# Context and mask rows loaded and masked one round earlier, in four buffers instead of two

## The chip, the core and the metric

The kernel runs on one core of a Trainium2 chip. The core has five engines with instruction streams of their own: TensorE (PE; its weight loads are shown apart as PEld), VectorE (DVE), ScalarE (ACT), GpSimd (POOL) and SyncE (SP). Here SyncE issues all transfers (DMA) between the device's memory and the core's own memory, SBUF. The engines wait for each other by semaphores. The metric is the device time of one execution in microseconds (us).

## What is computed

Sixteen sequences of 128 channels by 256 positions pass four layers, each added to its input:

```python
x = x + _L0_xattn_ref(ctx, ctx, _layernorm(x), ssm_kernel, D, 8)      # long convolution of key-value products
x = x + _L0_ffn_ref(_layernorm(x), gate_w, gate_b, val_w, val_b, out_w, out_b)   # quantised gated FFN
x = x + _L1_xattn_ref(_layernorm(x), ctx, mask, mask, Wq, bq, Wk, bk, Wv, bv)    # masked cross attention, 16 heads
x = x + _L1_ffn_ref(_layernorm(x), Wc, temperature, genes, Wd, Wu, norm_w, scale)  # top 32 of 512, weighted sum
```

The change concerns the third layer. Keys and values are projections of the context `ctx`, and positions are masked:

```python
q = einsum('oc,bct->bot', Wq, target) + bq
k = einsum('oc,bcs->bos', Wk, source) + bk
v = einsum('oc,bcs->bos', Wv, source) + bv
dot = mask * (q . k / sqrt(HEAD_DIM)) - (1 - mask) * NEG
out = (softmax(dot) * mask) @ v
```

The kernel multiplies the context with the mask row once (`ctx_m`), and takes the biases times the mask.

## The kernel before, in words

A first part prepares weights and begins the long convolution. Then every engine runs a loop over `m`. In each pass an engine does one step of many stages, each for another batch: the first stages for batch `m`, the last ones for batch `m - 12`. The order of the calls in each engine's loop is written out by hand, and an engine executes strictly in that order; a step that waits holds all behind it. The outer products of the convolution (`later_products`, L886, with L273 on TensorE) still run in the passes until about 205 us.

The way of batch `b` through the context steps, before the change:

- SyncE, `load_context(m - 6)`: after `write_attention` (L753) and `load_max_rows` (L742) of its pass, it issues the load of the context into `ctx_m[b % 2]` (L694) and of the mask row, spread over 128 partitions, into `mask_b[b % 2]` (L695). SyncE's passes run ahead of the others by about one. At the end of its pass stand `load_stacked_qk` (L726 to L735) and `load_x` (L686).
- GpSimd, `mask_context(m - 5)`: waits for both loads and multiplies them in place (L985). It stands between `chosen_weights` (L1027) and `output_scale`, ahead of `gate_times_value` (L963, two halves).
- TensorE, `project_qk(m - 5)`: keys from `ctx_m` (L432) and queries from the normalised x2 (L433), in the middle of its pass; at the end of the next pass `project_v(m - 6)` (L445, and L446 with the mask row).
- VectorE, `bias_and_mask_qk` (L1489, L1490): adds biases and applies the mask row, right behind `inverse_denominators` (L1510, L1512).
- GpSimd, `split_qk(m - 5)`: splits queries and keys into three bf16 parts (L39 to L45), after which come `add_attention` (L1011, L1013), `normalise_x1` (L910 to L915), `down_times_xr` (L1035) and `normalise_x3` (again L910 to L915).

Others that are named later: TensorE forms the products for the row maxima (L461), whose maxima VectorE takes (L1499), and the scores (L477), whose exponentials ScalarE takes (L1223). The rows of maxima go to the scores by a transfer (L742). TensorE transposes xq (L377, L378) and the normalised x3 (L511), and multiplies values (L490). VectorE opens the gate of the FFN (L1447). L963 needs this result.

Of the kernel before, what the change touches and what calls it, by code (L numbers as in the profile page):

```python
# [25 lines left out]
P = 128  # L26
# [21 lines left out]
def build(nc, a, out):  # L48
    B, C, L = a["x"].shape
# [4 lines left out]
    QB, UNITS = B // 4, 4 * H  # L54
    QK_SCALE = 1.0 / float(HD) ** 0.5
# [19 lines left out]
    with ExitStack() as ctx:  # L75
# [88 lines left out]
        ctx_m = [sb(f"ctx_m{k}", [P, L]) for k in range(2)]  # L164
        mask_b = [sb(f"mask_b{k}", [P, L]) for k in range(2)]
# [78 lines left out]
        def _(pe):  # L244
# [179 lines left out]
            def project_qk(b):  # L424
                if not live(b):
                    return
                if b == 0:
                    pe.wait_ge(s("w_T_taken"), 7)
                pe.wait_ge(s("ctx_m_ready"), b + 1)
                pe.wait_ge(s("xn2_ready"), b + 1)  # L430
                take6("qk", b)
                pe.matmul(X6[:, L:2 * L], wqkvT[:, 1, :], ctx_m[b % 2][:], start=True, stop=True)  # L432
                pe.matmul(X6[:, 0:L], wqkvT[:, 0, :], xn2, start=True, stop=True).then_inc(s("qk_bank_ready"), 1)  # L433

            def project_v(b):
# [7 lines left out]
                for sh in range(KL):  # L443
                    cols = slice(sh * P, (sh + 1) * P)
                    pe.matmul(X7[:, cols], ctx_m[b % 2][:, cols], wqkvT[:, 2, :], start=True, stop=False)  # L445
                    mm = pe.matmul(X7[:, cols], mask_b[b % 2][:, cols], bv0[:], start=False, stop=True)  # L446
# [150 lines left out]
        def _(sp):  # L597
# [90 lines left out]
            def load_context(b):  # L688
                if not live(b):
                    return  # L690
                if b >= 2:
                    sp.wait_ge(s("v_bank_ready"), b - 1)
                    sp.wait_ge(s("x6_free"), turn6["qk", b - 2])
                sp.dma_start(ctx_m[b % 2][:], a["ctx"][b]).then_inc(s(f"ctx{b % 2}_loaded"), 16)  # L694
                sp.dma_start(mask_b[b % 2][:], bass.AP(a["mask"].tensor, b * L, [[0, P], [1, L]])).then_inc(  # L695
                    s(f"ctx{b % 2}_loaded"), 16)
# [93 lines left out]
            for m in range(B + 14):  # L790
# [3 lines left out]
                load_context(m - 6)  # L794
# [6 lines left out]
                load_stacked_qk(m - 7)  # L801
                load_x(m)
# [5 lines left out]
        def _(pool):  # L808
# [171 lines left out]
            def mask_context(b):  # L980
                if not live(b):
                    return
                k = b % 2
                pool.wait_ge(s(f"ctx{k}_loaded"), 32 * (b // 2 + 1))
# [60 lines left out]
            for m in range(B + 12):  # L1045
# [7 lines left out]
                mask_context(m - 5)  # L1053
# [9 lines left out]
                split_qk(m - 5)  # L1063
                add_attention(m - 9)
# [256 lines left out]
        def _(dve):  # L1321
# [160 lines left out]
            def bias_and_mask_qk(b):  # L1482
                if not live(b):
                    return
                k = b % 2
# [159 lines left out]
```

## Time and profile before

| | |
|---|---|
| three runs | 626.14, 622.75, 619.33 us; median 622.75 |
| profiled execution | 624.76 us, span in the trace 622.9 us |
| mean granted TensorE clock | 0.923 of full speed |
| busy: PE | 489.1 us, 79% of the span |
| busy: DVE | 478.0 us, 77% |
| busy: POOL | 401.1 us, 64% |
| busy: ACT | 346.2 us, 56% |

The span is from the first to the last instruction of the trace, and the execution's own time lies 1.9 us above it. Busy shares are means over stages with different limits, so they don't tell by themselves what bounds the kernel. An idle time in brackets behind a row of the timeline is that just before the instruction, with what ended it. A granted clock of 1.00 is 2.4 GHz, 0.50 is 1.2 GHz, and values between are stretches with both.

### The profile page before, as it was taken

The numbers are of one execution on the slowest core, as the hardware profiler recorded it, in microseconds if no ns is written. First come the engines' busy times: TensorE is split into PE (matmuls) and PEld (weight loads), VectorE is DVE, ScalarE is ACT, GpSimd is POOL, SyncE is SP. The second block draws the span as 40 slices with busy tenths as digits, with TensorE's granted clock in tenths as the row PEclk, the third lists the DMA queues.
The fourth block names the chain that finished last, engine by engine and source line by source line (L and its number), as shares of the span: only waits on it lengthen the run. The fifth ranks groups of instructions, "written<-read, shape, count | busy, mean of one in ns | idle before, by whom it ended". The sixth has DMA issues, their size and how long they took to land.

```text
span 622.9 us, 11624 instructions
## 1 busy us (share of the span) xinstructions
PE 489.1 (79%) x3617; PEld 279.7 (45%) x3633; DVE 478.0 (77%) x885; ACT 346.2 (56%) x578; POOL 401.1 (64%) x711
## 2 busy tenths in 40 slices
PE   1676778888788788978989888899987987888463
PEld 1455656666565443444444444444433433333121
DVE  4563658888789876799999999999988868874441
ACT  1246723332221375777877878778865657776321
POOL 6787487798997567577787787785654643432321
PEclk9987979999998897999999999999988879997855
DMA  6940100020624155453563455455565454411100
GB/s 216 373 92 6 29 17 18 10 44 0 117 73 62 30 107 136 88 104 106 89 132 99 89 136 114 78 134 92 103 143 109 86 135 103 87 30 29 46 8 17
DMA packets 92178, 54.31 MB, mean 87 GB/s; under 512 B 14851, under 2 KB 91844, under 8 KB 92118
## 3 DMA queue, kind: packets, MB, share of 16 engines
q1 hardware_dynamic: 92118, 53.58, 38.4%
q8 instruction: 29, 0.48, 0.3%
q14 instruction: 31, 0.25, 0.1%
HBM read 35.64 MB, written 17.42 MB: 85 GB/s over the span
## 4 chain that ended last, share of the span: by engine, by line
POOL 22%; issue 22%; DVE 15%; DVEq 15%; PE 14%; POOLq 9%; ACT 2%; DMA 1%; SPq 0%; ACTq 0%
POOL kv L886 8%; DVE w_int L1499 4%; PE bank L490 3%; DVEq L1540 3%; DVEq L1550 2%; DVEq L1408 2%; POOL yT L843 2%; DVEq L1457 2%; DVE best L1551 2%; DVEq L1533 2%; POOL w_raw L963 2%; POOLq L914 2%; DVE st L1409 2%; DVEq L1436 2%; PE pair L477 1%
## 5 line engine op out<-in xcount | busy, mean ns | idle before, releaser
L1499 DVE TENSOR_REDUCE w_int<-pair 128x4 f32<-128x1024 f32 x128 | 155.6, 1216 | 17.2 <-PE pair L461 16.8
L1223 ACT ACTIVATE cT<-pair 128x1024 f32<-128x1024 f32 x128 | 130.9, 1023 | 57.2 <-PE pair L477 55.4
L273 PE MATMUL pair<-kv,toep 128*128 128x256 f32 x384 | 106.5, 420 | 29.5 <-POOL kv L886 15.3
L273 PEld LDWEIGHTS pair<-kv,toep 128*128 128x128 f32 x384 | 75.9, 209 | 50.3 <-issue 21.5
L886 POOL TENSOR_TENSOR kv<-cT 128x512 f32<-128x512 f32 x64 | 66.1, 1041 | 19.0 <-PE pair L273 12.9
L461 PE MATMUL pair<-KS,w_raw 54*128 54x256 bf16 x512 | 51.8, 282 | 29.6 <-DVE w_int L1499 29.4
L490 PE MATMUL bank<-cT,v_aug 128*32 128x256 f32 x1024 | 72.8, 405 | 0.0
L1361 DVE TENSOR_TENSOR prod<-pair,qT 128x512 f32<-128x512 f32 x64 | 44.3, 691 | 29.8 <-PE pair L273 25.0
L477 PE MATMUL pair<-w_raw,KS 57*128 57x256 bf16 x512 | 52.3, 284 | 13.0 <-ACT cT L1223 5.7
L461 PEld LDWEIGHTS pair<-KS,w_raw 54*128 54x128 bf16 x512 | 16.1, 96 | 73.4 <-DVE w_int L1499 59.8
L1368 DVE TENSOR_REDUCE yT<-prod 128x64 f32<-128x512 f32 x64 | 43.9, 686 | 6.3 <-issue 0.4
L1541 DVE MATCH_REPLACE8 toep<-best,toep 128x512 f32<-128x512 f32 x64 | 43.3, 676 | 0.6 <-issue 0.6
L1172 ACT ACTIVATE w_raw<-bank,st 128x512 f32<-128x512 f32 x32 | 22.0, 687 | 34.2 <-PE bank L383 34.2
L963 POOL TENSOR_TENSOR w_raw<-w_raw 128x512 f32<-128x512 f32 x32 | 40.3, 1275 | 0.0
L382 PE MATMUL bank<-wgvT,ctx_all 128*128 128x512 bf16 x112 | 35.6, 389 | 5.8 <-ACT ctx_all L1196 1.9
L1188 ACT ACTIVATE w_raw<-w_raw,st 128x512 f32<-128x512 f32 x32 | 21.3, 714 | 33.6 <-DVE st L1462 33.6
L477 PEld LDWEIGHTS pair<-w_raw,KS 57*128 57x128 bf16 x512 | 17.2, 96 | 50.5 <-ACT cT L1223 31.8
L490 PEld LDWEIGHTS bank<-cT,v_aug 128*32 128x32 f32 x1024 | 28.0, 113 | 26.1 <-issue 15.5
L1551 DVE MAX8 best<-toep 128x8 f32<-128x512 f32 x48 | 33.4, 695 | 4.2
L39 POOL CAST w_int<-w_int 128x512 bf16<-128x512 f32 (+1 forms) x32 | 13.1, 411 | 34.8 <-DVE w_int L1499 21.5
L519 PE MATMUL bank<-wcT,qT 128*128 128x512 f32 x64 | 34.1, 658 | 0.5 <-ACT qT L1237 0.5
L913 POOL TENSOR_TENSOR st<-st,half_neg 128x1 f32<-128x1 f32 x48 | 26.7, 555 | 7.0
(163 smaller groups left out, 996.1 us busy)
## 6 DMA issues: line engine op xcount, KB each, us to landing
w_raw<-scr_q SPq DMA_DIRECT2D x32, 192.0 KB
KS<-scr_k SPq DMA_DIRECT2D x32, 192.0 KB
scr_q<-w_int SPq DMA_DIRECT2D x16, 192.0 KB, 2.5
scr_k<-w_int SPq DMA_DIRECT2D x16, 192.0 KB, 2.6
scr_o<-qT SPq DMA_DIRECT2D x64, 36.0 KB
yT<-in_x SPq DMA_DIRECT2D x4, 512.0 KB, 7.4
ctx_all<-in_ctx SPq DMA_DIRECT2D x4, 512.0 KB, 7.8
x_b<-in_x SPq DMA_DIRECT2D x16, 128.0 KB, 5.2
```

Source lines behind the costliest of these rows:

```text
L273: mm = pe.matmul(bank[:, lh * n:(lh + 1) * n], toep[:, h, (lh - sh) * P:(lh - sh + 1) * P], rhs[:, sh, :], start=(sh == 0), stop=(sh == lh))
L461: mm = pe.matmul(M[:, at:at + L], QS[b % 3][rows, g, th * P:(th + 1) * P], KS[b % 3][rows, g, :], start=True, stop=True)
L477: mm = pe.matmul(SC[:, at:at + L], KS[b % 3][rows, g, sh * P:(sh + 1) * P], QS[b % 3][rows, g, :], start=True, stop=True)
L490: mm = pe.matmul(O[32 * jj:32 * jj + 32, 0:L], v_aug[b % 2][:, sh, 4 * q + jj, :], probs[(2 * q + jj // 2) % 4][:, jj % 2, sh * L:(sh + 1) ...
L886: pool.tensor_tensor(kv[u % 2][:], ch.unsqueeze(3).broadcast_to(shape), ch.unsqueeze(2).broadcast_to(shape), ALU.mult).then_inc(s("kv_read ...
L963: pool.tensor_tensor(h, h, val[half], ALU.mult).then_inc(s("hid_ready"), 1)
L1223: act.activation(probs[g % 4].rearrange("p j l -> p (j l)"), SC[:], ACT.Exp).then_inc(s("scores_free"), 1)
L1361: dve.tensor_tensor(prod[:], banks[2 + u % 2][:].rearrange("p (r j i) -> p r j i", j=HD, i=HD), qh.unsqueeze(2).broadcast_to([P, KL * QB, ...
L1368: mm = dve.tensor_reduce(yT[:, q].rearrange("p s b c -> p (s b) c")[:, :, heads], prod[:], AX.X, ALU.add)
L1499: dve.tensor_reduce(neg_max[:, :, 2 * g:2 * g + 2].rearrange("p t j -> p j t"), M[:].rearrange("p (j t s) -> p j t s", t=KL, s=L), AX.X, A ...
L1541: mm = dve.match_replace(left, best[:, 8 * r:8 * r + 8], logits[b % 2] if r == 0 else left, GONE)
L1551: dve.max(best[:, 8 * r:8 * r + 8], left)
```

## The change

Context and mask row get four buffers each. The load moves to the end of SyncE's pass, before `load_x`, and is for batch `m - 4` instead of `m - 6`. The mask product moves on GpSimd from ahead of the third outer product to behind `split_qk`, and is for batch `m - 4` instead of `m - 5`. The waits before the load and before the product are adapted to four buffers.

```diff
+    NC = 4
-        ctx_m = [sb(f"ctx_m{k}", [P, L]) for k in range(2)]
-        mask_b = [sb(f"mask_b{k}", [P, L]) for k in range(2)]
+        ctx_m = [sb(f"ctx_m{k}", [P, L]) for k in range(NC)]
+        mask_b = [sb(f"mask_b{k}", [P, L]) for k in range(NC)]
...
             def load_context(b):
                 if not live(b):
                     return
-                if b >= 2:
-                    sp.wait_ge(s("v_bank_ready"), b - 1)
-                    sp.wait_ge(s("x6_free"), turn6["qk", b - 2])
-                sp.dma_start(ctx_m[b % 2][:], a["ctx"][b]).then_inc(s(f"ctx{b % 2}_loaded"), 16)
-                sp.dma_start(mask_b[b % 2][:], bass.AP(a["mask"].tensor, b * L, [[0, P], [1, L]])).then_inc(
-                    s(f"ctx{b % 2}_loaded"), 16)
+                k = b % NC
+                if b >= NC:
+                    sp.wait_ge(s("v_bank_ready"), b - NC + 1)
+                    sp.wait_ge(s("x6_free"), turn6["qk", b - NC])
+                sp.dma_start(ctx_m[k][:], a["ctx"][b]).then_inc(s(f"ctx{k}_loaded"), 16)
+                sp.dma_start(mask_b[k][:], bass.AP(a["mask"].tensor, b * L, [[0, P], [1, L]])).then_inc(
+                    s(f"ctx{k}_loaded"), 16)
...
                 load_max_rows(m - 9)
-                load_context(m - 6)
                 load_denominator_masks(m - 7)
...
                 load_stacked_qk(m - 7)
+                load_context(m - 4)
                 load_x(m)
...
             def mask_context(b):
                 if not live(b):
                     return
-                k = b % 2
-                pool.wait_ge(s(f"ctx{k}_loaded"), 32 * (b // 2 + 1))
+                k = b % NC
+                pool.wait_ge(s(f"ctx{k}_loaded"), 32 * (b // NC + 1))
                 pool.tensor_tensor(ctx_m[k][:], ctx_m[k][:], mask_b[k][:], ALU.mult).then_inc(s("ctx_m_ready"), 1)
...
                 chosen_weights(m - 11)
-                mask_context(m - 5)
                 later_products(m - 2, 3)
...
                 split_qk(m - 5)
+                mask_context(m - 4)
                 add_attention(m - 9)
```

The readers of the buffers (`project_qk`, `project_v`, `bias_and_mask_qk`) take `b % NC` instead of `b % 2`. The line numbers of the changed kernel are higher by up to two.

GpSimd's order in the pass in which batch 4 is projected, before (L955 ends the scales of x, L963 are the two halves of gate times value, L39 to L45 the split, L1011 the attention sum):

```order
L955 TENSOR_TENSOR s_0<-st,s_0 128x1
L985 TENSOR_TENSOR ctx_m<-ctx_m,mask_b 128x256
L969 TENSOR_SCALAR st<-st,gammas 128x1
L937 TENSOR_SCALAR ctx_all<-ctx_all,st 128x256
L963 TENSOR_TENSOR w_raw<-w_raw 128x512 x2
L39 CAST w_int<-w_int 128x512
L41 TENSOR_TENSOR w_int<-w_int 128x512
L43 CAST w_int<-w_int 128x512
L45 TENSOR_TENSOR w_int<-w_int 128x512
L1011 TENSOR_TENSOR qT<-qT 128x256
```

The same place after the change, with the lines two higher:

```order
L957 TENSOR_TENSOR s_0<-st,s_0 128x1
L971 TENSOR_SCALAR st<-st,gammas 128x1
L939 TENSOR_SCALAR ctx_all<-ctx_all,st 128x256
L965 TENSOR_TENSOR w_raw<-w_raw 128x512 x2
L39 CAST w_int<-w_int 128x512
L41 TENSOR_TENSOR w_int<-w_int 128x512
L43 CAST w_int<-w_int 128x512
L45 TENSOR_TENSOR w_int<-w_int 128x512
L987 TENSOR_TENSOR ctx_m<-ctx_m,mask_b 128x256
L1013 TENSOR_TENSOR qT<-qT 128x256
```

The product has moved from ahead of gate times value to behind the split, and it is the next batch's.

SyncE's order from the load of x on, before (L753 writes the attention's result, L742 loads rows of maxima):

```order
L735 DMA KS<-scr_k 48x8x256
L686 DMA x_b<-in_x 128x256
L753 DMA scr_o<-qT 9x4x256 x4
L742 DMA w_raw<-w_int 3x8x256 x2
L694 DMA ctx_m<-in_ctx 128x256
L695 DMA mask_b<-in_mask 128x256
L765 DMA den_0<-scr_o 128x1x32
L767 DMA qT<-scr_o 128x1x256
```

And after:

```order
L737 DMA KS<-scr_k 48x8x256
L696 DMA ctx_m<-in_ctx 128x256
L697 DMA mask_b<-in_mask 128x256
L687 DMA x_b<-in_x 128x256
L755 DMA scr_o<-qT 9x4x256 x4
L744 DMA w_raw<-w_int 3x8x256 x2
L767 DMA den_1<-scr_o 128x1x32
L769 DMA qT<-scr_o 128x1x256
```

The two loads stand ahead of the load of x, and behind the rows of maxima the attention's loads follow directly.

## Rows read from the trace of the kernel before

**Rows 1.** Busy us (instructions) of PE, PEld, DVE, ACT, POOL; clock, DMA share, GB/s.
```profile
312.00:410.00 98.00, 86.25 (x767) 43.76 (x767) 91.47 (x174) 75.25 (x131) 74.37 (x147) 1.00 0.50 106
```

**Rows 2.** Waits of GpSimd: us in total, times, longest us.
```profile
POOL ctx_m L985 <- DMA mask_b<-in_mask: 15.2, 7, 2.5
```

**Rows 3.** Timeline of SyncE: start us, us, operation [idle before <-releaser].
```profile
224.25 0.47 SPq L686 DMA_DIRECT2D x_b<-in_x  x1
...
236.27 0.42 SPq L695 DMA_DIRECT2D mask_b<-in_mask  x1
```

**Rows 4.** Instructions on the tile mask_b: its transfers.
```profile
DMA to landing us min/median/max: 3.0/3.1/4.4
```

**Rows 5.** Timeline of GpSimd, rounds 4 and 7: the mask product.
```profile
239.82 0.72 POOL L985 TENSOR_TENSOR ctx_m<-ctx_m,mask_b 128x256 f32<-128x256 f32 x1 [2.48 <-DMA mask_b<-in_mask]
...
312.27 0.74 POOL L985 TENSOR_TENSOR ctx_m<-ctx_m,mask_b 128x256 f32<-128x256 f32 x1
```

**Rows 6.** Timeline of TensorE, round 3.
```profile
219.56 0.70 PE L432 MATMUL bank<-ctx_m,wqkvT 128*128 128x256 f32 x2 [0.72 <-POOL ctx_m L985]
...
222.60 0.39 PE L477 MATMUL pair<-w_raw,KS 57*128 57x256 bf16 x4
```

**Rows 7.** Timeline of TensorE, round 4.
```profile
240.60 1.22 PE L432 MATMUL bank<-ctx_m,wqkvT 128*128 128x256 f32 x2 [1.48 <-POOL ctx_m L985]
...
246.17 0.61 PE L477 MATMUL pair<-w_raw,KS 57*128 57x256 bf16 x4
```

**Rows 8.** The same view in stretches of rounds 4 and 14.
```profile
240.00:242.00 2.00, 1.40 (x3) 1.18 (x4) 0.60 (x3) 0.18 (x1) 2.00 (x4) 0.57 0.93 275
...
478.00:480.00 2.00, 1.52 (x12) 0.67 (x12) 1.93 (x5) 1.20 (x2) 0.00 (x0) 0.80 0.38 100
```

**Rows 9.** Timeline of VectorE, rounds 4 and 13.
```profile
247.25 1.23 DVE L1499 TENSOR_REDUCE w_int<-pair 128x4 f32<-128x1024 f32 x1 [2.52 <-PE pair L461]
...
460.29 0.48 DVE L1489 SCALAR_TENSOR_TENSOR w_int<-mask_b,bqk,bank 128x256 f32<-128x256 f32 x1 [0.96 <-PE bank L433]
...
465.99 1.23 DVE L1499 TENSOR_REDUCE w_int<-pair 128x4 f32<-128x1024 f32 x1 [0.87 <-PE pair L461]
```

**Rows 10.** L1512 (ns min/median/max; busy in a stretch), and its round 7.
```profile
L1512 DVE TENSOR_TENSOR den<-den,mask_all x16: 192/230/737, 240.5 to 584.3; 128x32 f32<-128x32 f32 x16
...
280.00:440.00 160.00, 3.96 (x7) 1.00 0.50 108
...
313.50 0.66 DVE L1447 SCALAR_TENSOR_TENSOR w_raw<-w_raw,bank 128x512 f32<-128x512 f32 x1
...
315.62 0.60 DVE L1512 TENSOR_TENSOR den<-den,mask_all 128x32 f32<-128x32 f32 x1
...
313.66 2.51 POOL L963 TENSOR_TENSOR w_raw<-w_raw 128x512 f32<-128x512 f32 x2
```

**Rows 11.** Timeline of TensorE, rounds 13, 14 and 15.
```profile
458.42 0.97 PE L432 MATMUL bank<-ctx_m,wqkvT 128*128 128x256 f32 x2 [1.10 <-POOL ctx_m L985]
...
480.94 1.22 PE L432 MATMUL bank<-ctx_m,wqkvT 128*128 128x256 f32 x2 [1.16 <-POOL ctx_m L985]
...
503.56 1.22 PE L432 MATMUL bank<-ctx_m,wqkvT 128*128 128x256 f32 x2 [1.10 <-POOL ctx_m L985]
...
508.39 0.61 PE L477 MATMUL pair<-w_raw,KS 57*128 57x256 bf16 x4
```

**Rows 12.** Timelines of GpSimd and TensorE where the product goes, two rounds.
```profile
299.94 0.73 POOL L1035 TENSOR_TENSOR toep<-qT 128x256 f32<-128x256 f32 x1 [0.16 <-ACT qT L1282]
300.89 0.19 POOL L910 TENSOR_SCALAR st<-st 128x1 f32<-128x1 f32 x1 [0.22 <-DVE st L1411]
...
302.22 0.55 POOL L915 TENSOR_SCALAR qT<-qT,st 128x256 f32<-128x256 f32 x1 [0.19 <-issue]
...
303.28 0.38 PE L511 MATMUL bank<-ident,qT 128*128 128x128 f32 x2
...
514.28 0.73 POOL L1035 TENSOR_TENSOR toep<-qT 128x256 f32<-128x256 f32 x1 [2.14 <-ACT qT L1282]
```

More of the change, by code:

```diff
@@ L431, in project_qk @@
                 take6("qk", b)
-                pe.matmul(X6[:, L:2 * L], wqkvT[:, 1, :], ctx_m[b % 2][:], start=True, stop=True)
+                pe.matmul(X6[:, L:2 * L], wqkvT[:, 1, :], ctx_m[b % NC][:], start=True, stop=True)
                 pe.matmul(X6[:, 0:L], wqkvT[:, 0, :], xn2, start=True, stop=True).then_inc(s("qk_bank_ready"), 1)
@@ L444, in project_v @@
                     cols = slice(sh * P, (sh + 1) * P)
-                    pe.matmul(X7[:, cols], ctx_m[b % 2][:, cols], wqkvT[:, 2, :], start=True, stop=False)
-                    mm = pe.matmul(X7[:, cols], mask_b[b % 2][:, cols], bv0[:], start=False, stop=True)
+                    pe.matmul(X7[:, cols], ctx_m[b % NC][:, cols], wqkvT[:, 2, :], start=True, stop=False)
+                    mm = pe.matmul(X7[:, cols], mask_b[b % NC][:, cols], bv0[:], start=False, stop=True)
                 mm.then_inc(s("v_bank_ready"), 1)
@@ L1484, in bias_and_mask_qk @@
                     return
-                k = b % 2
+                k = b % NC
                 dve.wait_ge(s("qk_bank_ready"), b + 1)
```

## The prediction

> **What bounds the kernel now.** I name a round by the batch whose queries and keys TensorE projects in it (L432, L433). The spans of the rounds come from the timeline of L432. First I read the chain of waits. It runs on GpSimd while the convolution lasts (to about 205 us), changes between GpSimd, TensorE and ScalarE up to round 5, then stays on VectorE to round 12 and from round 13 on is mixed again. In the VectorE stretch that engine is busy for 91.47 of 98 us [rows 1], and the rest lies between its instructions, so there a wait on another engine costs nothing. Then I read the waits: GpSimd stands before the mask product L985 for 15.2 us in 7 rounds, always for the mask row's transfer [rows 2]. In the timeline these are rounds 3, 4, 5 and 12 to 15. The reason is the order of SyncE, for round 4: the load is issued at 236.27, lands about 3.1 us after its issue, and GpSimd starts the product at 239.82 after 2.48 us of idle [rows 3, 4, 5]. Behind it TensorE stands idle at L432, 0.72 to 1.48 us long in rounds 3, 4, 13, 14 and 15 [rows 6, 7, 11]. Those idles, not the 15.2 us, are what the path can get back.
>
> **The wait goes.** The change issues the load of a batch in front of the load of x, which stands at 224.25 while the product that needs it comes one round later [rows 3], so at least 15 us lie between them where 3.1 are needed. Four buffers are free by then: the wait is on the value projection of four batches before. The two issues that leave the middle of SyncE's round (0.42 us and a little less) let its other work come up to 0.9 us earlier, and x come as much later. The cover of the second is that x is added only in the middle of the next round, over ten microseconds after its issue; without it 0.9 us a round would be due. I cost both at nothing.
>
> **What the path gets back, round by round.** These are the terms.
> - Round 3: TensorE idles 0.72 us before L432 [rows 6]. VectorE waits for TensorE right behind, so **0.72**.
> - Round 4: 1.48 us of idle [rows 7]. The granted clock then falls (0.57 in 240 to 242 us [rows 8]), that is to the 1.2 GHz level. From L432 to the second L477 behind it TensorE needs 246.17 - 240.60 = 5.57 us; the same instructions at 2.4 GHz in round 3 took 222.60 - 219.56 = 3.04 [rows 6, 7]. Difference 2.53. The idle in question lies directly at the fall, and before 238 us TensorE was nearly always busy, so I count the clock as kept: 1.48 + 2.53 = **4.01**. VectorE can follow: at one place behind it alone it waited 2.52 us for TensorE [rows 9], and at L1489 about as long.
> - Rounds 5 and 12: GpSimd waits, but VectorE is the later one. **0**.
> - Rounds 6 to 12: here nobody waits for the transfer. But the small VectorE product L1512, which takes 192 ns at best, took 3.96 us in seven rounds [rows 10]. At 315.62 it lasted 0.60 us and ended when GpSimd's two products L963 ended (313.66 + 2.51 = 316.17). The mask product, 0.74 us long at 312.27, stands in front of those [rows 5, 10]. Without it the first L963 ends near 314.2, and the second waits for VectorE's L1447, ready at 313.50 + 0.66 = 314.16, and ends near 315.4, before L1512 begins. Then L1512 is not held: 3.96 - 7 x 0.19 = **2.63** on the engine that bounds these rounds. Bounds: 0 (it meets L963 still) and 2.63; I take the upper one, since the orders of both engines are the same in all seven rounds.
> - Round 13: 1.10 us of idle [rows 11]. The clock falls there too, but VectorE, on which the chain goes on, waited only 0.96 and 0.87 us for TensorE [rows 9], so the whole gain is at most 1.83. TensorE had waited for others also. I take **1.10**.
> - Round 14: 1.16 us [rows 11]. The clock had fallen already within 478 to 480 us (0.80 [rows 8]), before the idle at L432, so I count none of it: **1.16**. If it stays up, up to 1.8 more.
> - Round 15: 1.10 us, and 508.39 - 503.56 = 4.83 us where round 3 needed 3.04 with two transposes more [rows 6, 11]: 1.79. Sum **2.89**.
>
> **The product in its new place.** Behind the split of query and key it delays what GpSimd does next by 0.74 us: the attention sum, the LayerNorm of x1, L1035 and the normalisation L915 of x3. In the rounds of VectorE, GpSimd waited 0.16 us before L1035 and 0.22 before the next step; 0.36 are left. L915 ended at 302.22 + 0.55 = 302.77, TensorE took its result at 303.28 [rows 12]: 0.51 of room. So 0. In the late rounds GpSimd waits before L1035 anyway (2.14 us in round 15 [rows 12]); at worst 0.4 us of the clock's part of round 15 goes back here. In the convolution rounds there are three mask products before the last outer product, before and after, and the fourth falls into a wait for the maxima in which it has room. So 0.
>
> **Two rules beside the rows.** L1512 has two inputs in SBUF, and so has L963 on the other engine; its long runs end with L963 [rows 10]. The Trainium skill, SBUF — State Buffer, on the engine side and its shared port pair, says that a VectorE instruction with two SBUF inputs and a GpSimd instruction that reads SBUF exclude each other for the whole instruction. By that rule, the trace agrees, the same rule would speak against the change if the product met such an instruction in its new place; there VectorE runs reductions with one input, and the sum stays.
> For the clock: in round 14 the rows show the fall ahead of the idle, in round 4 at it. The Trainium skill, TensorE: Matmul & The Clock Gate, part 1, says that the engine is slowed after it has been idle and released by sustained work; taken alone it would give back the clock of rounds 13 and 14 as well, which is the second case below.
>
> **Sum.** 0.72 + 4.01 + 2.63 + 1.10 + 1.16 + 2.89 = 12.51 us. The profiled execution took 624.76 us (span 622.9): 612.25. It lies 2.0 us above the median of the three runs, which themselves spread over 6.8 us, so I forecast **612.3** for the median and let the range carry the rest.
>
> **The cases.**
> - Forecast, 612.3: 0.38.
> - All of the clock comes back, also in rounds 13 (0.7) and 14 (1.8): 609.8. For it: the holes are filled. Against: row 478 to 480. 0.14.
> - The clock falls just the same, since TensorE still waits for VectorE and for the rows of maxima in these rounds: 12.51 - 2.53 - 1.79 = 8.19, 616.6. 0.16.
> - As that, and L1512 is held by something else of GpSimd: 5.56, 619.2. 0.12.
> - The next input is as late as the one removed. In rounds 13 to 15 the rows of maxima (a transfer, for which TensorE waited too) and the exponentials set the pace, and in round 4 the clock falls as before; only rounds 3 and 4 pay, 0.72 + 1.48 = 2.2: 622.6. 0.07.
> - The change does not do what it says, because SyncE reaches the load only behind a late transfer: 624.8. The 12 us between the load of x and the old place of the issue [rows 3] speak against it. 0.05.
> - **Slower.** In rounds 6 to 12 the product pushes L915 past the point at which TensorE wants it. It decides from a delay over 0.51 us. The late transposes hold the projections and the products behind them, the hole at that place grows by 0.23 us, which alone would be 1.6 us, and the clock falls in every round as it does in round 4: 7 x 2.53 = 17.7. With 5.56 gained elsewhere: 624.76 - 5.56 + 17.7 = 636.9. For it: these holes exist already. Against: 0.36 against 0.51, and a granted clock of 1.00 over the stretch [rows 1, 10]. 0.08.
>
> One per cent is 6.2 us, about what a measurement of this kernel can tell from no change: the bounds are 616.5 and 629. Faster by over 1%: the first two cases and more than half of the third, 0.62. Slower 0.08, the rest 0.30. The range reaches from 608 (all the clock, and a median below the profiled run) to 620.5 (holes only, L1512 held, and a little); outside lie the two cases of next to no gain, the slower one and a little luck below.
>
> **What would show it.** Right: no wait for in_mask at the mask product; no idle of TensorE before L432 from GpSimd; L1512 near 0.19 us in every round; VectorE's rounds some 0.4 us shorter; granted clock 1.00 behind L432 in round 4 and round 15. Wrong: L1512 still 0.6 us; a fall of the clock near the same places; TensorE waiting at L511 for GpSimd in rounds 6 to 12; GpSimd still waiting for a transfer at the product. If the time stays above 618, the clock's terms or L1512's have failed, and the traces tell which.

## The result and the profile after

The changed kernel takes 616.98 us (median of 10 runs, 612.53 to 618.73) where the kernel before takes 623.62 beside it (10 runs, 619.33 to 626.14): ratio 0.9896, 95% interval 0.9863 to 0.9928, so 1.0% faster and surely not slower. The forecast was 612.3 us, with a range of 608 to 620.5. The profiled execution took 617.04 us (span 615.0) against 624.76 (span 622.9); 7.9 us of span are there to be explained, where 12.51 were forecast. All ratios below leave out two executions in a slower state with a lower mean clock (633.22 us of the kernel before, 627.58 of the change's second series), which the medians and run counts still contain.

The waits of GpSimd first (us in total, times, longest), the first two of the changed kernel, and the instructions of its mask product. The mask row's transfer of [rows 2] is not in the list, and the view of L987 names nobody that its 16 products waited for.

```profile
POOL qT L1013 <- DMA qT<-scr_r: 31.3, 6, 8.9
POOL w_int L39 <- DVE w_int L1492: 24.8, 13, 5.0
```
```profile
L987 POOL TENSOR_TENSOR ctx_m<-ctx_m,mask_b x16: 723/727/733, 133.0 to 483.4; 128x256 f32<-128x256 f32 x16
```

The timeline of SyncE shows the two loads right in front of that of x (L687, at 225.68), where [rows 3] had twelve microseconds between x and the mask row:

```profile
224.74 0.42 SPq L696 DMA_DIRECT2D ctx_m<-in_ctx  x1
225.20 0.43 SPq L697 DMA_DIRECT2D mask_b<-in_mask  x1
```

To place the 7.9 us I lay the second projection product of each round, which is behind every wait of [rows 6, 7, 11], side by side. The timeline of TensorE (start, duration, operation), batches 0, 3, 5, 12 and 15, before:

```profile
148.65 0.59 PE L433 MATMUL bank<-ctx_all,wqkvT 128*128 128x256 f32 x2
...
220.10 0.59 PE L433 MATMUL bank<-ctx_all,wqkvT 128*128 128x256 f32 x2
...
265.38 0.59 PE L433 MATMUL bank<-ctx_all,wqkvT 128*128 128x256 f32 x2
...
436.21 0.59 PE L433 MATMUL bank<-ctx_all,wqkvT 128*128 128x256 f32 x2
...
504.57 1.06 PE L433 MATMUL bank<-ctx_all,wqkvT 128*128 128x256 f32 x2
```

and after:

```profile
147.67 0.59 PE L434 MATMUL bank<-ctx_all,wqkvT 128*128 128x256 f32 x2
...
222.37 0.59 PE L434 MATMUL bank<-ctx_all,wqkvT 128*128 128x256 f32 x2
...
264.21 0.59 PE L434 MATMUL bank<-ctx_all,wqkvT 128*128 128x256 f32 x2
...
433.70 0.59 PE L434 MATMUL bank<-ctx_all,wqkvT 128*128 128x256 f32 x2
...
497.50 0.59 PE L434 MATMUL bank<-ctx_all,wqkvT 128*128 128x256 f32 x2
```

The differences of these starts are the ledger; a negative gain is a loss. Ahead of batch 0 the twelve profiles of this document spread over 146.8 to 149.8 us and behind batch 15 over 115.5 to 118.7 us, without a pattern that I could read, so I read nothing into these two rows. Of the clock's 1.79 us that the forecast gave to round 15, 0.47 lie ahead of the start of L433 (504.57 - 503.56 = 1.01, where round 3 has 220.10 - 219.56 = 0.54) and 1.32 behind it, in the last row.

| stretch (start of one batch to start of the other) | before | after | gain | forecast |
|---|---|---|---|---|
| up to batch 0 | 148.65 | 147.67 | 0.98 | 0 |
| 0 to 3 (most of it convolution) | 71.45 | 74.70 | **-3.25** | 0.72 (round 3) |
| 3 to 5 | 45.28 | 41.84 | 3.44 | 4.01 |
| 5 to 12 | 170.83 | 169.49 | 1.34 | 2.63 |
| 12 to 15 | 68.36 | 63.80 | 4.56 | 3.83 |
| behind batch 15 | 118.3 | 117.5 | 0.8 | 1.32 |

From batch 0 to batch 15 that is 6.1 us; the other 1.8 of the 7.9 lie at the two ends. The late rounds pay a little more than forecast, the rounds of VectorE half, and 3.25 us are lost in a place that I had costed at nothing.

**The loss.** Timelines of TensorE and GpSimd between the projections of batches 0 and 1, before:

```profile
162.56 1.56 PE L273 MATMUL pair<-kv,toep 128*128 128x256 f32 x6 [2.67 <-POOL kv L886]
...
161.47 1.04 POOL L886 TENSOR_TENSOR kv<-cT 128x512 f32<-128x512 f32 x1
...
166.84 0.73 POOL L985 TENSOR_TENSOR ctx_m<-ctx_m,mask_b 128x256 f32<-128x256 f32 x1
```

and after:

```profile
161.88 2.93 PE L274 MATMUL pair<-kv,toep 128*128 128x256 f32 x6 [2.95 <-POOL kv L888]
...
156.16 0.73 POOL L987 TENSOR_TENSOR ctx_m<-ctx_m,mask_b 128x256 f32<-128x256 f32 x1
...
160.78 1.04 POOL L888 TENSOR_TENSOR kv<-cT 128x512 f32<-128x512 f32 x1
...
166.50 1.04 POOL L888 TENSOR_TENSOR kv<-cT 128x512 f32<-128x512 f32 x1 [0.32 <-PE pair L274]
```

In both kernels TensorE stands still for nearly 3 us here until GpSimd's next outer product kv. Before, the mask product came behind that hole, and TensorE started its next convolution products there without a wait for it. After, it is in the stretch of GpSimd's work that ends the hole (156.16), and the 0.73 us that it leaves behind the hole turn into waits of GpSimd for TensorE (0.32 at 166.50, four more such up to 192 us). The hole grew from 2.67 to 2.95 us, and the first products behind it took 2.93 us instead of 1.56. The windows of TensorE show the clock behind it (us, busy, granted clock, DMA share, GB/s), before and after:

```profile
162.00:166.00 4.00, 3.44 (x16) 1.00 0.84 146
186.00:190.00 4.00, 3.52 (x17) 1.00 0.71 136
```
```profile
162.00:166.00 4.00, 4.00 (x13) 0.64 1.16 174
186.00:190.00 4.00, 4.00 (x15) 0.65 1.22 161
```

In these two profiles the clock fell behind the hole in both of the first rounds of the change, and in neither of before. Only the hole's length goes with the place, though. It is 2.95 to 2.98 us in all four profiles with the early products at the new place and nothing in the hole, and 2.62 to 2.67 in the six with them at the old place. The fall in 162 to 166 us is found with either: the kernel with all products at the old place has it too, and loses next to nothing by it (the first experiment below):

```profile
162.00:166.00 4.00, 3.70 (x11) 0.57 0.88 164
```

In round 3 it is a matter of when the clock falls. TensorE waits for VectorE's reduction ahead of the last convolution products, before and after:

```profile
204.94 0.39 PE L461 MATMUL pair<-KS,w_raw 54*128 54x256 bf16 x4 [1.81 <-DVE w_int L1499]
...
206.49 0.61 PE L462 MATMUL pair<-KS,w_raw 54*128 54x256 bf16 x4 [3.29 <-DVE w_int L1501]
```

Timeline of VectorE behind that, before and after, its reductions L1499 and L1501:

```profile
205.38 1.23 DVE L1499 TENSOR_REDUCE w_int<-pair 128x4 f32<-128x1024 f32 x1 [0.49 <-PE pair L461]
...
207.98 1.23 DVE L1499 TENSOR_REDUCE w_int<-pair 128x4 f32<-128x1024 f32 x1 [0.20 <-PE pair L461]
```
```profile
207.14 1.23 DVE L1501 TENSOR_REDUCE w_int<-pair 128x4 f32<-128x1024 f32 x1 [0.71 <-PE pair L462]
...
210.54 1.23 DVE L1501 TENSOR_REDUCE w_int<-pair 128x4 f32<-128x1024 f32 x1 [1.00 <-PE pair L462]
```

In these two waits VectorE loses 1.71 us to TensorE instead of 0.69; the difference of 1.02 is close to the 1.07 us that round 3 became longer. TensorE before and after in windows of 198 to 202 us and from 206 us on:

```profile
198.00:202.00 4.00, 3.63 (x17) 0.66 0.00 0
...
206.00:210.00 4.00, 4.00 (x14) 0.57 0.00 0
```
```profile
198.00:202.00 4.00, 2.06 (x14) 1.00 0.00 0
...
206.00:210.00 4.00, 3.51 (x12) 0.50 0.00 0
210.00:214.00 4.00, 4.00 (x20) 0.67 0.00 0
```

Before, part of the slow time lay in 198 to 202 us, where VectorE was the later engine and TensorE only filled its idle time with it. After, all of it lies behind 206 us, where VectorE waits for TensorE.

**The rounds of VectorE.** Round 7 after, which answers to [rows 10], VectorE and GpSimd; then L1514 (was L1512) in the stretch of 280 to 440 us:

```profile
314.33 0.19 DVE L1514 TENSOR_TENSOR den<-den,mask_all 128x32 f32<-128x32 f32 x1
...
311.67 2.54 POOL L965 TENSOR_TENSOR w_raw<-w_raw 128x512 f32<-128x512 f32 x2
```
```profile
280.00:440.00 160.00, 2.17 (x7) 1.00 0.53 107
```

GpSimd's two products L965 end at 314.21, before L1514 begins at 314.33, and L1514 takes 0.19 us. That is the mechanism of the forecast. But 2.17 us in seven are not 7 x 0.19 = 1.33: one is left, in round 11 (another takes 0.23).

```profile
410.86 0.98 DVE L1514 TENSOR_TENSOR den<-den,mask_all 128x32 f32<-128x32 f32 x1
...
409.30 2.49 POOL L965 TENSOR_TENSOR w_raw<-w_raw 128x512 f32<-128x512 f32 x2
```

There VectorE has no x to add (L1423) and no statistics (L1411, L1413) between its MAX8 and L1449, since the last batch's x is through, and comes to L1514 while L965 runs: L1514 ends at 411.84, L965 at 411.79. The Trainium skill, SBUF — State Buffer, section Who interferes with whom, has the shared port pair as an exclusive lock for the whole instruction; both rows agree with it, the one that escapes and the one that is caught.

**Rounds 4 and 13 to 15.** In round 4 TensorE waits 0.18 us before L433 instead of 1.48, at a clock of 1.00 where [rows 8] had 0.57:

```profile
241.57 0.67 PE L433 MATMUL bank<-ctx_m,wqkvT 128*128 128x256 f32 x2 [0.18 <-ACT w_raw L1182]
...
246.09 0.39 PE L478 MATMUL pair<-w_raw,KS 57*128 57x256 bf16 x4 [0.82 <-ACT cT L1225]
```
```profile
240.00:242.00 2.00, 1.58 (x13) 0.66 (x11) 1.93 (x4) 2.00 (x4) 1.95 (x3) 1.00 0.80 235
```

The row at 246.09 is the third L478 behind L433. TensorE comes to the second after 244.58 - 241.57 = 3.01 us, as the forecast had it (3.04); from there on it waits for others, as the filled holes below show.

In round 13 no product waits for GpSimd either, and the clock falls all the same: L433 takes 1.22 us behind two short waits, the first for the transfer of the rows of maxima.

```profile
453.16 0.39 PE L478 MATMUL pair<-w_raw,KS 57*128 57x256 bf16 x4 [1.15 <-DMA w_raw<-w_int]
...
454.67 0.39 PE L478 MATMUL pair<-w_raw,KS 57*128 57x256 bf16 x4 [0.31 <-ACT cT L1225]
454.99 1.22 PE L433 MATMUL bank<-ctx_m,wqkvT 128*128 128x256 f32 x2
```

### The profile page after: what moved, and what is told of

It is laid out like the page before. It is cut to its first block, busy times and chain, and to the rows that moved or that the text cites. A ratio compares the mean times of both kernels' runs of the same rounds, so it can differ in the third digit from the quotient of the medians.

```text
span 615.0 us, 11622 instructions
## 1 busy us (share of the span) xinstructions
PE 486.1 (79%) x3617; PEld 280.0 (46%) x3633; DVE 476.3 (77%) x885; ACT 345.8 (56%) x578; POOL 400.2 (65%) x711
## 4 chain that ended last, share of the span: by engine, by line
POOL 22%; issue 21%; DVE 15%; DVEq 15%; PE 13%; POOLq 12%; ACT 1%; SPq 0%; DMA 0%; ACTq 0%
POOL kv L888 7%; DVE w_int L1501 4%; DVEq L1542 3%; PE pair L274 3%; POOLq L914 3%; POOL w_raw L965 3%; PE bank L491 2%; POOL yT L845 2%; DVEq L1552 2%; DVEq L1459 2%; POOLq L916 2%; DVEq L1410 2%; DVE best L1553 2%; POOLq L42 2%; DVEq L1513 2%
## 5 line engine op out<-in xcount | busy, mean ns | idle before, releaser
L1501 DVE TENSOR_REDUCE w_int<-pair 128x4 f32<-128x1024 f32 x128 | 155.6, 1216 | 18.5 <-PE pair L462 18.2
L274 PE MATMUL pair<-kv,toep 128*128 128x256 f32 x384 | 109.7, 430 | 28.0 <-POOL kv L888 14.5
L274 PEld LDWEIGHTS pair<-kv,toep 128*128 128x128 f32 x384 | 78.6, 216 | 48.5 <-issue 20.4
L478 PE MATMUL pair<-w_raw,KS 57*128 57x256 bf16 x512 | 51.8, 282 | 15.8 <-DMA w_raw<-w_int 7.0
L462 PEld LDWEIGHTS pair<-KS,w_raw 54*128 54x128 bf16 x512 | 15.8, 95 | 74.1 <-DVE w_int L1501 62.1
L965 POOL TENSOR_TENSOR w_raw<-w_raw 128x512 f32<-128x512 f32 x32 | 40.6, 1270 | 2.7 <-DVE w_raw L1449 1.6
L39 POOL CAST w_int<-w_int 128x512 bf16<-128x512 f32 (+1 forms) x32 | 13.1, 409 | 44.4 <-DVE w_int L1492 24.8
L478 PEld LDWEIGHTS pair<-w_raw,KS 57*128 57x128 bf16 x512 | 17.1, 96 | 52.2 <-ACT cT L1225 33.2
L520 PE MATMUL bank<-wcT,qT 128*128 128x512 f32 x64 | 32.2, 627 | 0.5 <-ACT qT L1239 0.5
L1013 POOL TENSOR_TENSOR qT<-qT 128x256 f32<-128x256 f32 x16 | 11.6, 727 | 31.4 <-DMA qT<-scr_r 31.3
```

Of the source, the lines that this page charges most:

```text
L274: mm = pe.matmul(bank[:, lh * n:(lh + 1) * n], toep[:, h, (lh - sh) * P:(lh - sh + 1) * P], rhs[:, sh, :], start=(sh == 0), stop=(sh == lh))
L462: mm = pe.matmul(M[:, at:at + L], QS[b % 3][rows, g, th * P:(th + 1) * P], KS[b % 3][rows, g, :], start=True, stop=True)
L478: mm = pe.matmul(SC[:, at:at + L], KS[b % 3][rows, g, sh * P:(sh + 1) * P], QS[b % 3][rows, g, :], start=True, stop=True)
L965: pool.tensor_tensor(h, h, val[half], ALU.mult).then_inc(s("hid_ready"), 1)
L1501: dve.tensor_reduce(neg_max[:, :, 2 * g:2 * g + 2].rearrange("p t j -> p j t"), M[:].rearrange("p (j t s) -> p j t s", t=KL, s=L), AX.X, A ...
```

## The experiments

The first theory: the early load does all the good of rounds 4, 5 and 13 to 15; the product's new place costs in the convolution and pays in rounds 6 to 12, so that the two can be had apart. The rival: the early load itself, its transfers or the four buffers cost in the convolution. Results (ratio to the kernel before on the same chip as recorded, which can differ by up to 0.2% from the quotient of the medians; the four stretches are from the profiled execution, as in the ledger):

| kernel | median us (runs) | ratio, 95% interval | 0 to 3 | 3 to 5 | 5 to 12 | 12 to 15 |
|---|---|---|---|---|---|---|
| before | 623.6 to 624.2 | 1 | 71.45 | 45.28 | 170.83 | 68.36 |
| the change | 616.98 (10) | 0.9896 [0.9863, 0.9928] | 74.70 | 41.84 | 169.49 | 63.80 |
| the change again | 617.46 (9) | 0.9890 [0.9856, 0.9924] | 74.13 | 41.87 | 169.80 | 62.87 |
| all at the old place | 615.47 (6) | 0.9844 [0.9790, 0.9898] | 71.37 | 42.18 | 170.85 | 62.36 |
| the same again | 615.00 (6) | 0.9855 [0.9811, 0.9898] | 71.37 | 41.74 | 170.81 | 62.35 |
| old place, three buffers | 615.56 (6) | 0.9871 [0.9826, 0.9916] | 71.41 | 41.77 | 170.93 | 62.36 |
| hybrid | 613.48 (6) | 0.9841 [0.9802, 0.9881] | 70.78 | 42.59 | 169.57 | 62.35 |
| hybrid again | 614.43 (6) | 0.9845 [0.9805, 0.9885] | 72.29 | 41.86 | 169.54 | 62.38 |
| early ones only | 616.51 (6) | 0.9874 [0.9828, 0.9919] | 74.68 | 41.72 | 172.07 | 62.41 |
| product back | 617.48 (7) | 0.9894 [0.9857, 0.9931] | 74.16 | 41.83 | 172.06 | 62.42 |
| filled boundary | 615.99 (4) | 0.9864 [0.9815, 0.9913] | 73.66 | 41.87 | 169.57 | 65.38 |
| filled hole (of before) | 620.41 (12) | 0.9962 [0.9928, 0.9996] | 72.35 | 43.75 | 172.04 | 67.96 |

### All products at the old place, loads early

```
                 chosen_weights(m - 11)
+                mask_context(m - 5)
                 later_products(m - 2, 3)
...
-                mask_context(m - 4)
```

> Loads early and four buffers as in the change, but the mask product at its old place on GpSimd (for the batch projected in the same round, ahead of gate times value). Theory: the wait for the transfer is gone, so rounds 13 to 15 gain as in the change (about 4.6 us) and rounds 3 and 4 as well (3 to 4 us); L1512 of VectorE is held by L963 as before (0.4 to 0.7 us in rounds 6 to 12), these rounds stay 24.8 us long, and 2.1 us of the change's gain are missing there. The convolution rounds 1 to 3, which in the change lost 3.3 us to a falling clock, keep their length of before (22.1, 22.6, 26.8 us) if the new place of the product made them longer. Time 615 to 617. Rival (the early load itself disturbs rounds 1 to 3): they are as long as in the change, and the time is 619 to 620.

Measured: 615.47 us, and the stretch of batches 0 to 3 is back at 71.37. L1514 is held again, 3.56 us in the seven rounds of 280 to 440 us:

```profile
280.00:440.00 160.00, 3.56 (x7) 1.00 0.51 107
```

So the loads and the buffers cost the convolution nothing, and the place alone costs it 3 us. The clock was at 0.57 in 162 to 166 us here too (0.79 and 0.57 in the other two kernels of this kind), and rounds 1 and 2 together still take 44.7 to 44.9 us in the three, where before has 44.66: the fall in round 1 is not what the change lost. Rounds 13 to 15 gain 6.0 us, more than expected. In round 13 the clock stays up (1.00 in 452 to 456 us); L433 takes 0.70 us.

```profile
453.72 0.70 PE L433 MATMUL bank<-ctx_m,wqkvT 128*128 128x256 f32 x2
```

### Hybrid: the first three at the old place, the others at the new

```
+                if m - 5 < 3:
+                    mask_context(m - 5)
                 later_products(m - 2, 3)
...
-                mask_context(m - 4)
+                if m - 4 >= 3:
+                    mask_context(m - 4)
```

> The change, but in the convolution rounds (batches 0 to 2) the mask product stands at its old place between the outer products, and from batch 3 on at the new one. Theory (the new place widens TensorE's hole at the boundary of the convolution rounds, and the clock falls): rounds 1 to 3 as long as before, rounds 6 to 12 at 24.4 us, rounds 13 to 15 as in the change: 613 to 614, 3 us less than the change. Rival (the clock falls of the convolution are chance): 616 to 617, as the change.

Measured: 613.48 us, and 614.43 the second time. It keeps the gain of rounds 5 to 12 (169.57 and 169.54 us), and in the first profile it loses nothing before (70.78). Its second profile has 72.29 in the first stretch: the clock fell to 0.65 in 186 to 190 us there, with the product at the old place, so a fall in round 2 is not only the new place's doing. The expected 70.8 to 71.5 us of that stretch were missed by it; the 2.5 to 3.5 us below the change beside it came (617.46 - 614.43 = 3.0).

> The hybrid once more (mask product at its old place for batches 0 to 2, at the new one from batch 3 on). Rounds 1 to 3 sum up to 70.8 to 71.5 us, and it is 2.5 to 3.5 us faster than the change beside it. Rival (the first comparison was luck): no difference beyond 1 us.

### Early ones only, the mirror image

```
+                if m - 5 >= 3:
+                    mask_context(m - 5)
                 later_products(m - 2, 3)
...
-                mask_context(m - 4)
+                if m - 4 < 3:
+                    mask_context(m - 4)
```

> The mirror image of the hybrid: the products of batches 0 to 2 behind the split of query and key, as in the change, those of batches 3 to 15 at their old place. Theory (the new place costs in the convolution rounds and pays only in rounds 6 to 12): rounds 1 to 3 take 73.7 to 74.7 us as in the change, L1514 is held again (0.57 to 0.74 us) and rounds 6 to 11 take 24.8 us each; this is the worst of the four combinations, 2.5 to 3.5 us above the kernel with all products at the old place, about 618 us. Rival (what is lost in rounds 1 to 3 is given back later, because VectorE bounds the rounds behind): the difference is there at round 3 and gone by round 12, about 615.5 us.

Measured: 616.51 us; 74.68 in the first stretch as in the change, 172.07 from 5 to 12, 1.2 more than the 170.8 of the old place. Of this, 0.84 are the small product (L1517 here), which is held for 1.28 us in round 11 of this profile (0.44 in the old-place kernels). The neighbour:

> All products at the old place with the early load, a second time, beside its neighbour on the same chip: rounds 1 to 3 take 71.0 to 71.7 us, rounds 4 and 5 42.2, rounds 13 to 15 62.4, 615 us. If both theories of the first kernel are wrong and the place of the early products costs nothing in time, the two come out within 1 us of each other.

Measured: 615.00 us. The difference to its neighbour is 1.5 us in the medians, less than the forecast 2.5 to 3.5 and with intervals that overlap; in the profiled spans it is 5.3 us (615.3 and 610.0), of which 3.31 and 1.26 are the two stretches. With the hybrids this makes a square: the first stretch takes 74.1 to 74.7 us with the first three products at the new place, in four profiles, and 70.8 to 72.3 at the old, in five (71.45 before); the stretch of 5 to 12 takes 169.5 to 169.8 with the others at the new place and 170.8 to 172.1 at the old.

### An extra product at the old place, in rounds 6 to 12

```
+                if 6 <= m - 5 <= 12:
+                    pool.tensor_tensor(wc_raw[:, 2, :], wc_raw[:, 0, :], wc_raw[:, 1, :], ALU.mult)
                 later_products(m - 2, 3)
```

> The change, with an extra product of the same size (128 x 256, on data that nothing reads) at the old place of the mask product in the rounds 6 to 12. Theory (L1512 of VectorE is held by GpSimd's L963, which this pushes back by 0.73 us): L1512 takes 0.6 us again in these rounds, each is 24.8 us instead of 24.4, and the kernel is 2 to 3 us slower than the change: 619 to 620. Rival (the rounds became shorter since no transfer or other work of GpSimd lies there): L1512 0.19 us, time 617.

Measured: 617.48 us. It is the change with the removed delay put back, and in the stretch of 280 to 440 us the small product (L1516 here) is busy for

```profile
280.00:440.00 160.00, 4.37 (x7) 1.00 0.51 106
```

instead of 2.17. Each of the rounds from 6 to 10 lasts 24.77 or 24.78 us instead of 24.40 or 24.41, so 0.37 per round, where the hold is 0.57 - 0.19 = 0.38. In this engine's rounds a hold of VectorE is paid in full. The 2 to 3 us that I expected of the whole kernel did not show: its median is 0.5 us above the change's. The 2.3 to 2.6 us of this stretch are less than the runs of one kernel differ by (615.3 to 618.7), and the profile's last stretch is 1.4 us shorter than in the change, as the clock did not fall in round 13.

### The holes of the kernel before, filled

One (batch 3) or two (4, 13, 14, 15) matmuls into a free bank in front of the wait for the mask product; nothing of them is used.

```
                 if b == 0:
                     pe.wait_ge(s("w_T_taken"), 7)
+                if b in (3, 4, 13, 14, 15):
+                    for _ in range(1 if b == 3 else 2):
+                        pe.matmul(O[:, L:2 * L], wqkvT[:, 0, :], wcT[:, 0, 0:L], start=True, stop=True)
                 pe.wait_ge(s("ctx_m_ready"), b + 1)
```

> The kernel before, with one or two matrix products into an unused half of a bank ahead of TensorE's wait for the masked context, in rounds 3 (one), 4, 13, 14 and 15 (two each, about 1.1 us at full clock). They fill the idle without shortening the wait. Theory (the idle before L432 is what lets the clock fall): the granted clock stays at 1.00 behind L432 in rounds 4 and 15 at least, the stretch from L432 to the second L477 behind it falls from 5.6 and 4.8 us to 3.0 and 2.6, and 4 to 6 us are gained though GpSimd waits for the transfer as before: 618 to 620. Rival (the clock falls by the low activity before, whatever stands in this hole): same stretches at 0.50, time 623 to 625.

Measured: 620.41 us, 0.4% under before, just above the 618 to 620 of the theory. The clock is 1.00 in 216 to 222 and 240 to 242 us, and the round from 4 to 5 lasts 22.56 us instead of 23.76: 1.20 us, not the 2.53 that I had put on the clock. The rows of TensorE and VectorE behind it:

```profile
239.75 0.70 PE L435 MATMUL bank<-ctx_m,wqkvT 128*128 128x256 f32 x2 [0.57 <-POOL ctx_m L988]
...
244.29 0.39 PE L480 MATMUL pair<-w_raw,KS 57*128 57x256 bf16 x4 [0.90 <-ACT cT L1226]
```
```profile
243.44 1.23 DVE L1502 TENSOR_REDUCE w_int<-pair 128x4 f32<-128x1024 f32 x1 [0.51 <-PE pair L464]
```

TensorE's own rows return the 2.53: it comes to the second L480 3.03 us behind L435 (242.78 - 239.75; 5.57 before). VectorE's reduction comes 2.5 us earlier as well, counted from the start of L433 (3.15 us behind it instead of 5.63). Half of it is lost further on in the round, in waits for the other engines. TensorE waits for ScalarE's exponentials (0.90 us at 244.29, 0.69 at the same place before; they take 1.02 us each, whatever TensorE's clock is) and for GpSimd's normalisation at the transposes (0.55 us, none before), and one later wait of VectorE for TensorE is 2.56 us long instead of 1.79. The change shows the same (0.82 before L478 at 246.09, 0.56 at the transposes, 2.57).

Over all sixteen batches nothing is left of it. From batch 0 to batch 15 this profile takes 356.10 us, the kernel before 355.92. Counted from L433 to L433 and named by the batch at their end, rounds 4, 5, 14 and 15 are 0.3, 1.2, 0.8 and 0.8 us shorter. Round 3 is 0.8 and round 13, where the clock had fallen already before the filling, 1.2 us longer. Rounds 6 to 12 are another 1.2 longer, with L1515 (the small product here) held for up to 1.23 us. The 0.4% of the medians can't be put down to the clock, then.

### The hole of the convolution in the change, filled

```
                 value(m - 2, 0)
+                if 5 <= m <= 7:
+                    for _ in range(4):
+                        pe.matmul(O[:, L:2 * L], ones[:], toep[:, 0, :], start=True, stop=True)
                 later_convolve(m - 2, 0)
```

> The change, with four extra matrix products (about 0.43 us each at full clock) on TensorE ahead of the first convolution product of the passes 5, 6 and 7, where it waits 2.9 us for GpSimd's outer product. Theory (the product in its new place makes this hole longer, and the clock that falls behind it is what rounds 1 to 3 lost): granted clock 1.00 from 150 to 195 us, rounds 1 and 2 (from the projection of batch 0 to that of batch 2) together at most 45.2 us instead of 46.8 in the change and 44.7 before. Rival (the loss is GpSimd's own 0.73 us per pass, whatever the clock): the two rounds stay at 46.3 to 46.8 us with a clock of 1.00. Round 3 is not touched and stays near 27.8 us.

Measured: 615.99 us, not to be told from the change. Its windows of TensorE over the two places where the change's clock was 0.64 and 0.65, and over round 3:

```profile
162.00:166.00 4.00, 3.09 (x15) 1.00 0.59 140
...
186.00:190.00 4.00, 4.00 (x21) 1.00 1.12 178
...
206.00:210.00 4.00, 3.16 (x10) 0.55 0.00 0
```

The clock is up in the first two rounds, and these take 45.58 us together: 1.26 and 0.67 less than in the two profiles of the change (46.84, 46.25), and 0.92 more than before (44.66). That is neither the theory's 45.2 at most nor the rival's 46.3 to 46.8. So of what rounds 1 and 2 lose, 0.9 us stays with the clock up, which I put down to GpSimd's longer way to the end of the hole, and the rest is the clock. Round 3 is as long as in the change (28.08 us, 27.86 there, 26.79 before), because its fall is another one. The clock fell in round 13 too (0.50 in 456 to 460 us), which is why the last stretch takes 65.38 us.

### Controls

The change once more, on the chip of the second set, and a variant with three buffers, the load one iteration ahead and the product at the old place:

> The change itself, once more, beside the hybrid below on the same chip. Rounds 1 to 3 sum up to 74.2 to 74.7 us again, if their length is the kernel's and not chance; rounds 4 to 15 as before within 1.5 us but for the clock. Time 616 to 618.

Measured: 617.46 us, with the same falls in 186 to 190 (0.64) and behind 206 us; in 162 to 166 us the clock was 1.00 this time. Rounds 1 to 3 take 74.13 us, a little under the expected 74.2 to 74.7.

```
+    NC = 3
...
-                load_context(m - 6)
...
+                load_context(m - 5)
                 load_x(m)
```

> Three buffers instead of four, the load at the end of SyncE's pass for one batch less ahead (m - 5), the mask product at its old place. The load is then issued about 12 us ahead of the product where 3.1 are needed, and the value projection of three batches before has ended by then. Theory (the place of the load in the queue matters, not the number of buffers beyond three): as the kernel with the product at its old place and four buffers, 614 to 616; no wait for the mask row's transfer. Rival (SyncE stands before the load for the buffer and holds the load of x): a wait of GpSimd or VectorE for a transfer in most rounds, time 618 or more.

Measured: 615.56 us, and no wait for the mask row's transfer. Three buffers and half the lead do what four do.

## Why the prediction was in its range and 4.7 us too low

**The wait goes, as forecast.** No product waits for its row, and the next transfer is not late.

**The step that failed: "In the convolution rounds there are three mask products before the last outer product, before and after, and the fourth falls into a wait for the maxima in which it has room. So 0."** I counted products and not where each stands to TensorE's hole. Their number is the same; but each of them moved from behind the hole, where TensorE had work for as long, to the front of it. It costs 3.25 us (2.7 in the second profile) against the kernel before, and 3.3 (2.8) against the kernels at the old place. Some 0.9 stays when the hole is filled, 0.7 to 1.3 went with the filling of it, and 1.07 is round 3. Round by round, counted in the same way, and without the two kernels with filled holes (in brackets the number of profiles):

| us | new place, clock up | new place, clock fallen | old place, clock up | old place, clock fallen |
|---|---|---|---|---|
| round 1 (162 to 166 us) | 22.34, 22.37 | 22.90, 24.38 | 22.01 to 22.06 (3) | 22.54 to 22.73 (3) |
| round 2 (186 to 190 us) | 23.15 | 23.88 to 23.95 (3) | 22.18 to 22.60 (5) | 23.35 |
| round 3 | | 27.15 to 27.88 (4) | | 26.23 to 26.88 (6) |

With the clock alike, then, the new place costs some 0.3 us in round 1 (the 24.38 I can't explain) and 0.5 to 1.0 in round 2, and a fall costs 0.7 to 1.2 in round 2. Whether the new place makes a fall likelier isn't shown: there are two falls of four against three of six in round 1, and three of four against one of six in round 2. The chain of waits, which I had read as GpSimd's in these rounds, said where to look first: 0.73 us moved on the engine that bounds a stretch.

**Round 3: 0.72.** With the product at the old place rounds 1 to 3 together take 71.4 us, as before (71.45); round 3 itself is 0.14 to 0.33 us shorter. The idle was removed, and the path got at most half of it. I take it that VectorE has the rest, which no run isolates.

**Round 4: 1.48 + 2.53.** Rounds 4 and 5 give 3.44 us. The forecast was right for TensorE: 3.01 us in the change between the instructions for which I had 3.04, and 5.57 before. What failed is that the path gets all of it: the filled holes return 1.20 us for the clock in that round, since ScalarE and GpSimd hold TensorE further on. The gain of 3.44 holds some of round 5, to which I gave 0.

**Rounds 6 to 12: 2.63.** The mechanism was right, the size was 1.34. Five rounds give 0.38 to 0.52 each, 2.09 together. The sixth is caught in the other way (0.98 us instead of 0.46, which is 0.5 of loss), and the first of the stretch has become 0.27 us longer in all kernels with the early load (23.91 to 23.94, once 24.18, where before has 23.64), old place or new. I take it that the lead of rounds 4 and 5 meets VectorE there. That "the orders of both engines are the same in all seven rounds" was false: in round 11 VectorE's queue is shorter by three instructions, as the x of the last batch is through.

**Rounds 13 to 15: 3.83 up to the start of L433 in batch 15, and 4.56 measured** (5.49 in the second profile), 6.0 in all kernels in which the clock stays up in round 13. There the clock of round 14, to which I gave 0 since it fell ahead of the idle, came back: it is 1.00 from 474 to 484 us in the first old-place kernel, whose batch 14 comes at 475.15, and 0.90 and 0.50 in 476 to 480 and 480 to 484 us before. So my case "all of the clock comes back, also in rounds 13 and 14" (2.5 us more) came nearly whole in these kernels, with 2.2. In the change the clock fell in round 13 in both profiles, behind a wait for the rows of maxima of 0.76 to 1.15 us, with no idle from GpSimd; it did in the kernel with the filled hole of the convolution too. What decides that fall I can't say: the kernel with the product put back, otherwise the change, waits 0.81 us there and kept the clock. Behind L433 of batch 15 TensorE reaches its sixth L478 in 8.92 us instead of 10.73, but the end comes only 0.8 us sooner, which is within the spread of that row.

**The rivals.** None came as written. The third case, a clock that falls just the same, had 616.6, and 616.98 were measured: that is a coincidence, since the clock of rounds 4 and 15 did come back. That the time lies in the stated range is in part luck as well: the range was wide enough for a loss in the convolution that no case had. The slower one, a clock that falls in each of rounds 6 to 12, did not come (1.00 in 280 to 440 us), but its mechanism, GpSimd's product that makes TensorE's hole longer, did, five rounds earlier than I had looked for it. TensorE's transposes L512 did not wait: 302.00 against an end of L917 at 301.81. The sum of the measured terms of the hybrid, 0 + 3.4 + 1.3 + 6.0 = 10.7, would be 614.1, and its medians are 613.5 and 614.4: with the failed step out, the forecast was 1 to 2 us off. Some of that closeness is chance, as the forecast for the median was taken from a profiled execution 2.0 us above the median of its three runs.

**What stays open.** The medians of the variants lie within 4 us of one another, and their intervals overlap, the change and the hybrid too (up to 0.9885 and from 0.9856); that the hybrid is the best rests on its two medians and on the stretches of the profiles, not on an interval that separates them. The ratio of the first old-place kernel (0.9844) equals the hybrids' (0.9841, 0.9845), and from batch 0 to batch 15 the profiles of the hybrid take 345.3 and 346.1 us, those of the three old-place kernels 346.3 to 346.8. Against before it is surely faster, by 1.2 to 2.0%. It is also not shown whether the fall behind 206 us comes from the lost time in the rounds before: all five profiles with the early products at the new place have it (0.50 to 0.65 in 206 to 210 us and 0.50 to 0.67 in 210 to 214), and the six with them at the old place, that of before among them, are back at 0.95 to 1.00 in 210 to 214.

## What to carry to other kernels

When an instruction is moved along an in-order queue, ask of each stretch on which side of the other engine's hole it stood and stands; the number of instructions up to some later point doesn't tell. A move that helps in one phase and costs in another can be made by phase, with a condition on the round: 3 us here. And price a fall of the clock by what reaches the end of the round: TensorE's own rows gave back the full 2.53 us here and the round 1.20, since the other engines held TensorE further on.

## What the runs showed of the hardware

- A VectorE product of 128x32 elements with two inputs in SBUF takes 0.19 us, and 0.43 to 1.28 us where it begins while one of GpSimd's two 128x512 products runs; in the rows shown it ends with them (411.84 and 411.79). A shift of 0.73 us in GpSimd's queue decided whether it was caught in rounds 6 to 10.
- The fall of TensorE's clock (1.00 to 0.50 in the windows) cost 1.2 us in round 4 and 0.7 to 1.2 in round 2. In 198 to 202 us, where TensorE had been waiting for VectorE, it seems to cost next to nothing, and behind 206 us 1.0; these two are read from the traces, not tested. Filling the idle in front with unused matmuls kept the clock at 1.00 in three of the four rounds in which it had fallen (4, 14 and 15; in round 13 it fell ahead of the filling). The sum of the rounds did not get shorter by it (356.10 us against 355.92).
- The same kernel had a fall in 162 to 166 us in one profile (0.64) and none in the other (1.00), so one profile doesn't tell a fall that comes always from one at the edge.
